# The l1 projection of a fused decoder kernel: keys first, then q and the third projection

## What is computed

```python
qk = x @ w_attn.T + b_attn
q, k = jnp.split(qk, 2, axis=-1)
scores = jnp.einsum('bhqd,bhkd->bhqk', q, k) * scale
scores = jnp.where(causal, scores, -jnp.inf)
y_ar = jnp.einsum('bhqk,bhkd->bhqd', jax.nn.softmax(scores, axis=-1), v)   # v is x itself
e = v[:, :, 1:, :] - y_ar[:, :, :-1, :]
q2 = q[:, :, 1:, :]
k2 = _heads(x[:, :-1] @ w_k2.T + b_k2)
qa = -jax.nn.leaky_relu(-q2 * scale, negative_slope=0.02)
ka = jax.nn.sigmoid(k2 * scale * 0.02)
ma = jnp.einsum('bhqd,bhkd->bhqk', qa, ka)      # lower triangle only
```

## Time and profile before

| | |
|---|---|
| time, median of 3 executions | 934.41 us (930.77 to 934.91) |
| span of the profiled execution, first to last instruction | 930.4 us |
| TensorE matmul busy | 829.7 us, 89% |
| VectorE, ScalarE, GpSimd busy | 712.0, 638.0, 299.9 us |
| mean granted TensorE clock | 0.975 |

### The profile page before, as it was taken

The page is one execution under the profiler, slowest core; times in us unless marked ns, Lnnn a source line. Parts: engine busy times, 40 slices in busy tenths (PEclk is TensorE's granted clock), DMA queues, the critical chain, the costliest instruction groups (busy, mean ns, idle before and its releaser), DMA issues.

```text
span 930.4 us, 29456 instructions
## 1 busy us (share of the span) xinstructions
PE 829.7 (89%) x11901; PEld 663.2 (71%) x11910; DVE 712.0 (77%) x1619; ACT 638.0 (69%) x2507; POOL 299.9 (32%) x554
## 2 busy tenths in 40 slices
PE   4576789999999999999999999999999999988873
PEld 3454567778778787878787787878787877766642
DVE  6886586878797888878787879788887878786442
ACT  2434668595968687786969686877869695847541
POOL 1121222233243434243333434342423333231221
PEclk8888999999999999999999999999999999999997
DMA  9300200000100000000001000000001000000000
GB/s 332 135 6 17 86 8 22 2 25 2 36 2 28 10 22 11 13 19 8 27 2 33 8 27 9 25 13 7 20 7 28 10 8 11 11 7 7 7 2 11
DMA packets 24440, 24.87 MB, mean 27 GB/s; under 512 B 2304, under 2 KB 22640, under 8 KB 24176
## 3 DMA queue, kind: packets, MB, share of 16 engines
q1 hardware_dynamic: 24304, 22.98, 7.6%
HBM read 18.80 MB, written 2.10 MB: 22 GB/s over the span
## 4 chain that ended last, share of the span: by engine, by line
PE 74%; ACT 14%; DVE 7%; issue 2%; POOL 2%; DMA 1%; SPq 0%; DVEq 0%; POOLq 0%; ACTq 0%
PE bank L1307 39%; PE s_tile L1307 26%; ACT prob L792 8%; PE bank L1428 3%; ACT k_ L825 3%; PE bank L1517 3%; DVE rope_ L1071 1%; ACT probT L731 1%; ACT cross_ L816 1%; PE bank L1547 1%; ACT xt_ L876 1%; DMA q_<-in_c_attn 1%; PE s_tile L1428 1%; DVE stats L1021 1%; POOL rstd L659 1%
## 5 line engine op out<-in xcount | busy, mean ns | idle before, releaser
L792 ACT ACTIVATE prob<-s_tile,low 128x128 f32<-128x128 f32 x768 | 272.5, 401 | 6.6 <-DVE low L1079 6.5
L792 ACT ACTIVATION_READ_ACCUMULATOR prob<-s_tile,low 128x1 f32 x768 | 185.9, 242 | 0.0
L1079 DVE TENSOR_REDUCE low<-s_tile 128x4 f32<-128x512 f32 x192 | 121.1, 680 | 18.4 <-PE s_tile L1307 18.4
L657 POOL TENSOR_TENSOR var_eps<-mean_var,rsq 128x1 f32<-128x1 f32 x144 | 31.0, 215 | 270.7 <-DVE mean_var L1023 270.7
L731 ACT ACTIVATE probT<-bank 128x512 f32<-128x512 f32 x192 | 99.4, 616 | 24.9 <-PE bank L1517 24.9
L659 POOL TENSOR_TENSOR rstd<-var_eps,rsq 128x1 f32<-128x1 f32 x144 | 87.1, 605 | 11.3
L731 ACT ACTIVATE xt_<-bank 128x256 f32<-128x256 f32 x64 | 24.5, 383 | 87.2 <-PE bank L1428 87.1
L1307 PE MATMUL bank<-w_gu,xt_ 128*128 128x352 f32 x256 | 78.4, 459 | 0.6 <-ACT xt_ L731 0.6
L694 POOL TENSOR_TENSOR k_<-q_,q_scale 128x256 f32<-128x256 f32 x32 | 19.8, 618 | 180.0 <-DVE q_ L982 180.0
L1517 PE MATMUL bank<-cst,prob 32*128 32x32 f32 x3072 | 61.4, 225 | 18.1 <-ACT prob L792 11.7
L1517 PEld LDWEIGHTS bank<-cst,prob 32*128 32x128 f32 x3072 | 54.0, 138 | 31.6 <-issue 14.8
(11 more groups left out here) (200 smaller groups left out, 1952.2 us busy)
## 6 DMA issues: line engine op xcount, KB each, us to landing
xtin<-in_xT SPq DMA_DIRECT2D x16, 128.0 KB, 2.3
next_<-in_x SPq DMA_DIRECT2D x16, 128.0 KB, 6.8
ct_<-in_ctxT SPq DMA_DIRECT2D x16, 128.0 KB, 7.5
w<-in_w SPq DMA_DIRECT2D x2, 1024.0 KB, 6.3
out<-x_ SPq DMA_DIRECT2D x16, 128.0 KB, 1.7
next_<-x_ SPq DMA_DIRECT2D x16, 127.0 KB
rowt<-in_rows SPq DMA_DIRECT2D x1, 1664.0 KB, 9.0
w<-in_gate_up SPq DMA_DIRECT2D x2, 512.0 KB, 6.3
```

The lines of the kernel that those rows point to most:

```text
L657: pool.tensor_tensor(var_eps[:, b:b + 1], mean_var[:, b, 1:2], rsq[:, 0:1], ALU.add) .then_inc(eps_in, 1)
L792: ins = act.activation(prob[:, r, c * P:(c + 1) * P], bank[r][:, c * P:(c + 1) * P], ACT.Exp, bias=low[:, b, at0:at0 + 1], accum_out=sums[ ...
L1079: dve.tensor_reduce(low[:, b, 4 * r:4 * r + 4], rows4(src[:, :]), AX_X, ALU.max, negate=True)\
```

## The change

TensorE and ScalarE both make the keys first; a new semaphore l1q_done tells of q, and the table COVERED is written anew, now as a mask with one bit for each tile. The core of the diff:

```diff
-    "l1_turn_x": ["xt"], "l1_project": ["qk2", "k"],
+    "l1_turn_x": ["xt"], "l1_project": ["k", "qk2"],
...
-    ("f0_up", "free.s0"): (0, 16), ("f0_up", "l0_project.qk"): (0, 16), ("f0_up", "x1_up.h0"): (0, 16),
...
-    ("l1_ma", "free.s2"): (0, 16), ("l1_ma", "free.s3"): (14, 16), ("l1_ma", "l0_lat.s0"): (0, 16),
...
-    ("l1_scores", "l1_project.k"): (0, 16), ("l1_scores", "x1_scores.s3"): (0, 16),
...
+    ("f0_turn_h2", "free.t1"): 0x8000, ("f0_turn_x", "free.xt"): 0x0001, ("f0_up", "free.s0"): 0xffff,
+    ("f0_up", "free.s1"): 0xffff, ("f0_up2", "f0_turn_x.xt"): 0xffff, ("f0_up2", "free.s2"): 0x0001,
...
+    ("l1_ma", "free.s0"): 0x7fff, ("l1_ma", "free.s1"): 0xffff, ("l1_ma", "free.s2"): 0xffff,
+    ("l1_ma", "free.s3"): 0xffff, ("l1_ma", "pairs_done"): 0xffff, ("l1_ma_value", "free.y"): 0xffff,
...
+    ("l1_project", "free.qk2"): 0x8000, ("l1_scores", "free.s0"): 0xffff, ("l1_scores", "free.s1"): 0xffff,
+    ("l1_scores", "free.s3"): 0xffff, ("l1_scores", "l1q_done"): 0xffff, ("l1_turn_x", "free.xt"): 0xffff,
...
-        e_done, masked = sem("e_done"), sem("masked")
+        e_done, masked, l1q_done = sem("e_done"), sem("masked"), sem("l1q_done")
...
             def l1_project(i, b):
+                keys = wait_full(act, i, ("l1_project", b, "k"))
+                emptied(by_halves(i, k_[:, b, :, :], keys, l1k_mb), i, ("l1_project", b, "k"))
                 src = wait_full(act, i, ("l1_project", b, "qk2"))
                 for m in range(KD):
-                    act.activation(q_[:, b, m, :], src[:, m * P:(m + 1) * P], ACT.Identity,
-                                   bias=col["l1qb"][:, m:m + 1])
-                keys = wait_full(act, i, ("l1_project", b, "k"))
-                emptied(by_halves(i, k_[:, b, :, :], keys, l1k_mb), i, ("l1_project", b, "k"))
+                    ins = act.activation(q_[:, b, m, :], src[:, m * P:(m + 1) * P], ACT.Identity,
+                                         bias=col["l1qb"][:, m:m + 1])
+                ins.then_inc(l1q_done, 1)
...
             def covered(stage, i, b, name):
-
-
-                first, last = COVERED.get((stage, name), (0, 0))
-                return i is not None and first <= i * GROUP + b < last
+                return i is not None and COVERED.get((stage, name), 0) >> (i * GROUP + b) & 1 == 1
...
                     elif layer == "l1":
                         need_empties(stage, i, [("l1_project", b, "k")])
+                        need(stage, i, b, "l1q_done", l1q_done, at("ACT", i, ["l1_project"], "l1_project", b))
...
             def l1_project(i, b):
-                dst = free(i, ("l1_project", b, "qk2"), [("l1_turn_x", b, "xt")])
+                dst = free(i, ("l1_project", b, "k"), [("l1_turn_x", b, "xt")])
+                filled(features(dst, w_l1, 2 * D, KD, xt_[:, b, :, :]), i, ("l1_project", b, "k"))
+                dst = free(i, ("l1_project", b, "qk2"))
                 filled(features(dst, w_l1, 0, 4, xt_[:, b, :, :]), i, ("l1_project", b, "qk2"))
-                dst = free(i, ("l1_project", b, "k"))
-                filled(features(dst, w_l1, 2 * D, KD, xt_[:, b, :, :]), i, ("l1_project", b, "k"))
```

More of the change, by code:

```diff
@@ L205 @@
 COVERED = {
[57 rows of a table removed]
+    ("f0_down", "free.o"): 0xffff, ("f0_turn_h", "free.t0"): 0x8002, ("f0_turn_h2", "dequant"): 0xffff,
+    ("f0_turn_h2", "free.t1"): 0x8000, ("f0_turn_x", "free.xt"): 0x0001, ("f0_up", "free.s0"): 0xffff,
+    ("f0_up", "free.s1"): 0xffff, ("f0_up2", "f0_turn_x.xt"): 0xffff, ("f0_up2", "free.s2"): 0x0001,
+    ("f0_up2", "free.s3"): 0x0001, ("f1_out", "f1_turn_x.xt"): 0x3fff, ("f1_out", "free.o"): 0xc9fa,
+    ("f1_turn_x", "free.xt"): 0xc000, ("l0_lat", "free.s0"): 0xfffe, ("l0_lat", "free.s1"): 0xfffe,
@@ new lines @@
+    ("l0_lat", "free.s3"): 0x000e, ("l0_lat", "l0_project.qk"): 0xfffe, ("l0_latent", "free.q"): 0x0003,
+    ("l0_mix0", "free.t0"): 0xffff, ("l0_mix0", "free.t1"): 0xffff, ("l0_mix0", "free.t2"): 0xfffc,
+    ("l0_mix0", "free.t3"): 0xffff, ("l0_mix0", "l0_scores.s2"): 0xffff, ("l0_mix1", "l0_scores.s3"): 0xffff,
+    ("l0_mix2", "l0_scores.s0"): 0xfffc, ("l0_out", "free.o"): 0xffff, ("l0_project", "free.qk"): 0x0002,
+    ("l0_scores", "free.s1"): 0xffff, ("l0_scores", "free.s2"): 0xffff, ("l0_scores", "free.s3"): 0x0003,
@@ new lines @@
+    ("l0_scores", "k_done"): 0xfff0, ("l0_scores", "l0_lat.s3"): 0x0003, ("l0_spread", "free.iv"): 0x0003,
+    ("l0_spread", "inverse"): 0xfffc, ("l0_v", "came_xT"): 0xffff, ("l0_v", "free.v"): 0xc42a,
+    ("l0_value", "free.y"): 0xffff, ("l0_value", "l0_mix0.t0"): 0xffff, ("l0_value", "l0_mix0.t1"): 0xffff,
+    ("l0_value", "l0_mix0.t3"): 0xffff, ("l0_value", "l0_v.v"): 0xfffe, ("l1_back", "free.yb"): 0xffff,
+    ("l1_ma", "free.s0"): 0x7fff, ("l1_ma", "free.s1"): 0xffff, ("l1_ma", "free.s2"): 0xffff,
@@ new lines @@
+    ("l1_ma", "free.s3"): 0xffff, ("l1_ma", "pairs_done"): 0xffff, ("l1_ma_value", "free.y"): 0xffff,
+    ("l1_ma_value", "l1_ma.s0"): 0xffff, ("l1_ma_value", "l1_ma.s1"): 0xffff, ("l1_ma_value", "l1_ma.s2"): 0xffff,
+    ("l1_ma_value", "l1_ma.s3"): 0xffff, ("l1_mix0", "free.t0"): 0xffff, ("l1_mix0", "free.t1"): 0xffff,
+    ("l1_mix0", "free.t2"): 0x8000, ("l1_mix0", "free.t3"): 0x7fff, ("l1_mix0", "l1_scores.s2"): 0xffff,
+    ("l1_mix1", "l1_scores.s3"): 0xfffc, ("l1_out", "free.o"): 0xffff, ("l1_out", "l1_ma_value.y"): 0x7fff,
@@ new lines @@
+    ("l1_project", "free.qk2"): 0x8000, ("l1_scores", "free.s0"): 0xffff, ("l1_scores", "free.s1"): 0xffff,
+    ("l1_scores", "free.s3"): 0xffff, ("l1_scores", "l1q_done"): 0xffff, ("l1_turn_x", "free.xt"): 0xffff,
+    ("l1_value", "free.y"): 0x0001, ("l1_value", "l1_mix0.t1"): 0xffff, ("l1_value", "l1_mix0.t2"): 0xffff,
+    ("l1_value", "l1_mix0.t3"): 0xffff, ("l1_value", "v_copied"): 0xffff, ("x0_attend", "free.o"): 0xfffe,
+    ("x0_attend", "x0_project.q"): 0x0001, ("x0_kv", "free.kv"): 0xfffe, ("x0_mix", "free.m"): 0xffff,
@@ new lines @@
+    ("x0_mix", "x0_kv.kv"): 0xffff, ("x0_project", "free.q"): 0xffff, ("x0_turn_x", "free.xt"): 0x0003,
+    ("x0_turn_x", "normed"): 0xfffe, ("x1_down", "free.o"): 0xffff, ("x1_down", "x1_up.h0"): 0x7fff,
+    ("x1_down2", "x1_up2.h1"): 0x0201, ("x1_keys", "came_ctx"): 0xffff, ("x1_keys", "free.k"): 0xffff,
+    ("x1_mix0", "free.t0"): 0xffff, ("x1_mix0", "free.t1"): 0x7fff, ("x1_mix0", "free.t2"): 0x4000,
+    ("x1_mix0", "free.t3"): 0xffff, ("x1_mix0", "x1_scores.s2"): 0xffff, ("x1_mix2", "x1_scores.s0"): 0xffff,
@@ new lines @@
+    ("x1_mix3", "x1_scores.s1"): 0xffff, ("x1_project", "free.q"): 0xffff, ("x1_scores", "free.s1"): 0xffff,
+    ("x1_scores", "free.s2"): 0xffff, ("x1_scores", "free.s3"): 0x0001, ("x1_scores", "x1_keys.k"): 0xffff,
+    ("x1_turn_h", "affine"): 0x1fff, ("x1_turn_h", "free.xt"): 0x8dea, ("x1_turn_x", "free.xt"): 0x8000,
+    ("x1_up", "free.h0"): 0xf000, ("x1_up", "x1_turn_h.xt"): 0x7fff, ("x1_up2", "free.h1"): 0x8000,
+    ("x1_value", "free.y"): 0xffff, ("x1_value", "x1_mix0.t0"): 0xffff, ("x1_value", "x1_mix0.t2"): 0xffff,
@@ L263 @@
+    ("x1_value", "x1_values.v"): 0xffff, ("x1_values", "came_ctx"): 0xffff, ("x1_values", "free.v"): 0xffff,
 }
```

## The result

The changed kernel takes 925.66 us (median of 9, 924.99 to 931.37), the kernel before, timed on the same chip, 933.22 us (9 executions, 930.45 to 934.91). The ratio is 0.9936, with an interval of 0.9919 to 0.9952: faster by 0.64%. A second series gave 926.39 us and 0.9949 (0.9933 to 0.9965). 929.4 us had been forecast, 0.54% under the median shown then.

What follows compares the result with a forecast made beforehand. TensorE's wait at l1_scores for ScalarE's tanh was taken to bound the tile path; 4.2 us from steady tiles plus 0.8 from the last, other edits 0, gave 934.4 - 5.0 = 929.4 us, 8-in-10 range 925.2 to 934.2.

Steps and rivals of the forecast that it cites:

- The place and the path: TensorE's wait at l1_scores falls from 16.2 to about 11.2 us; chain goes through norm and keys, not all 24 records.
- The steady tiles: ScalarE's pause before the keys closes in 15 tiles: TensorE restarts 0.24 us earlier, keeps 0.75 of its wait; 4.2 us gained.
- The last tile: With keys first, TensorE restarts the scores at 856.61 in place of 857.44: 0.8 us gained.
- The returned keys wait: Keys wait beside the bank-2 wait at l1_scores: taken as 0, since keys are done early; bound 0.8 us slower.
- The sum: Steady tiles' 4.2 us plus the last tile's 0.8 give 5.0 us gained.
- The left-out waits: 67 waits no longer issued: taken as 0, already fulfilled when TensorE came; worth at most 3.4 us gained.
- The end: Behind the last scores, where the clock falls, one slow stretch more or fewer moves the time 1.7 us either way.
- Taken back by the next wait: TensorE waits longer for ScalarE's exponentials (11.7 us, growing by 4), losing part or all: 931.9 to 934.4; chance 0.18.
- No pause to close: If one q takes 0.41 us start to start on ScalarE, both orders end alike: 933.6 us; chance 0.03.
- The clock: Fewer, longer TensorE waits drop its clock inside periods, 1.7 us per fall; in 8 tiles 943.0 us; chance 0.05.

Runs made afterwards that it cites:

- second series: The changed kernel, unedited, timed once more beside the follow-up kernels: 926.39 us, ratio 0.9949 to the kernel before.
- the order alone: Kernel before with keys first on TensorE and ScalarE, old table of covered waits, no keys wait at l1_scores, no l1q_done: 924.37 us, ratio 0.9927.
- without the double wait: Changed kernel with the keys wait taken out, so l1_scores waits for bank 2 alone: 925.42 us, ratio 0.9926.
- the old order: Kernel before, q still first, with the keys wait brought back at l1_scores ahead of the bank-2 wait: 936.23 us, ratio 1.0040.
- on one side alone: Kernel before with keys first on one engine only: TensorE only 947.52 us (1.0167), ScalarE only 946.70 us (1.0161).
- the three kernels with stalls of 1.08 and 1.51: Kernel before with the keys wait brought back (936.23 us), with keys first on TensorE only (947.52), and on ScalarE only (946.70).
- q on VectorE: Changed kernel with q written by VectorE, keys and q sharing bank 0, l1_scores waiting for both banks: 922.28 us, ratio 0.9897.

## Why the prediction was right

**The number.** The forecast of 0.54% lies within both intervals (0.48% to 0.81%, and 0.35% to 0.67%). The time itself was less well met, and there luck helped: 925.66 is 3.7 us under 929.4 and only 0.5 above the lower end of the range, 925.2. The 934.4 from which 5.0 was taken was the median of three executions; the same kernel's medians were 933.22 beside the changed kernel and 931.1 to 931.8 in the later series.

**The place and the path.** Right. The stall at the scores fell, the chain left the 24 records and went through the norm, and each tile shows keys, q, tanh in one run.

**The steady tiles.** 4.2 us were worked out, 0.24 to 0.28 for a tile, and a stall of 0.75. With the order alone the stall is 0.61 to 0.75 in tiles 1 to 14, and the period 50.48 against 50.76. In the changed kernel the stall is 0.70 to 0.84 and the period 0.23 shorter. The sum of TensorE's waits for the tanh was to fall to 11.2: it is 10.9 with the order alone and 12.4 in the changed kernel.

**The last tile.** 0.8 forecast; the stall fell by 0.79, from 0.99 to 0.21, and by 0.88 without the double wait.

**The returned keys wait.** This is the term that was mis-sized. I took 0, with 0.8 as its bound, because the keys are done long before. The wait that costs is not theirs. With two waits the compiler put the bank-2 wait, the late one, into the instruction of 51 ns, and the first matmul follows 0.09 us later than before: 0.144 against 0.053, in each of 16 tiles. That is 1.5 us of stall, and 1.0 to 1.2 us of time in the 13 clean periods. In the comparison with the order alone up to the last scores only 0.8 shows (755.3 against 754.5), because the left-out waits give some of it back. The rule of the Trainium skill (Perfetto Trace Analysis, Identifying Dependency Chains) was the right place to look; the cover I named hid the wrong one of the two waits.

**The sum.** 5.0 forecast. From the first projection to the last scores the order alone won 5.3 (759.8 to 754.5), the changed kernel 4.5, and 4.8 in its second series (755.0).

**The left-out waits.** 0 taken; the times show none, the profiles about 0.5 us. The two terms taken as 0 have opposite signs, which is luck: together they moved the sum by less than 1 us.

**The end.** The further 1.9 us of the profiled span come from two slow stretches of the clock that the profile before had behind the last scores, and this one had not. The prediction named 1.7 each as a term of either sign; these two cost about 1.0 each, and those of the steady part about 1.4. That is luck of the two executions and no part of the change. The first series has 7.6 between its medians, while the ratios say 0.64% and 0.51%; how much of that is due to such stretches is not shown.

**The rivals.** Taken back by the next wait: the wait for the exponentials went from 11.7 to 12.8, 1.1 and not 4. No pause to close: refuted by the pause's end. The clock: not in the changed kernel, but falls of the clock do happen at this place: they came in the old order when the stall grew from 0.99 to 1.08.

## What to carry to other kernels

Where one engine drains what another fills, look at the pause inside the drain, not at the sum of either, and change the order on both sides together; on one side alone it cost 1.6%. When an instruction gets a second wait, put the one that comes last in time first in the program, and see in the trace which of the two became an instruction of its own. A stall that grows a little can cost more than it is long, through the clock: look at the granted clock of the stretch behind it.

## What the runs showed of the hardware that was not expected

- Of two waits in front of a matmul, the one later in the program became the separate instruction. Where that was also the one fulfilled last, TensorE started 0.143 to 0.146 us behind the releasing instruction (three profiles). Where the other was last by 0.5 us or more, or there was one wait alone, it started 0.051 to 0.054 behind it (before and six more), the same in all 16 tiles. With q on VectorE the separate one was fulfilled 0.01 to 0.07 us before the other in 15 tiles, and the start still came 0.144 to 0.146 behind it.
- A stall 0.09 us longer in each tile (1.08 for 0.99) came with three stretches at 1.2 GHz in the steady part and 0.40% of time (3.7 us), where the stalls themselves are 1.4 us longer. The 11 such stretches in the steady part of the three kernels with stalls of 1.08 and 1.51 lie at the scores (from 0.14 us before their start to 1.7 behind it). Six more, in kernels with stalls of 1.00 and less, lie 10.5 to 11.5 us behind it, at the waits for the exponentials and their copies, and none of theirs at the scores. Why those come in some executions and not in others was not settled.
- Two neighbouring instructions on ScalarE start 0.25 us apart for q (128x128, bias alone) while one lasts 0.35 to 0.38, and 0.34 apart for the keys, which last 0.45. The distance of the starts, and not the duration, is what a chain on that engine costs.
